# Score and maximum pairs issued in runs of three, with a third score bank taken from the shared PSUM banks

## The reference

```python
# attention: 16 heads of 16, blocks of 128 tokens; a query block sees its own, the previous and the next block
scores = einsum('bhnqd,bhnkd->bhnqk', qb, kwin) * (1 / sqrt(256))
scores = where(|kpos - qpos| <= 128 and 0 <= kpos < 512, scores, -1e30)
out = softmax(scores) @ vwin; out = out @ Wout + bout
x = layernorm(x + out)
# feed-forward with weights rounded to -1, 0, 1
h = relu(x @ Wq1.T + b1)      # 256 -> 1024
x = layernorm(x + h @ Wq2.T + b2)
```

## Time and profile before

| | us |
|---|---|
| median of three runs (1227.03 to 1229.11) | 1227.82 |
| the profiled execution's own time | 1229.44 |
| its span | 1227.7 |
| granted TensorE clock, mean share of full speed | 0.927 |

### The profile page before, as it was taken

The page is one execution under the profiler, slowest core; times in us unless marked ns, Lnnn a source line. Parts: engine busy times, 40 slices in busy tenths (PEclk is TensorE's granted clock), DMA queues, the critical chain, the costliest instruction groups (busy, mean ns, idle before and its releaser), DMA issues.

```text
span 1227.7 us, 28104 instructions
## 1 busy us (share of the span) xinstructions
PE 1074.5 (88%) x8132; PEld 794.1 (65%) x8132; DVE 861.3 (70%) x2934; ACT 611.0 (50%) x1258; POOL 520.0 (42%) x824
## 2 busy tenths in 40 slices
PE   4778998989898899989899998998999899897956
PEld 3445666767666676766667676666767666675746
DVE  2977768777776777777677777768777776777433
ACT  4255545545454554555455454545545454554521
POOL 2233453435445343544534354453435445344430
PEclk8688899998989999898989989899998989899988
DMA  6644424444342444434244443424444342442000
GB/s 173 94 70 71 71 39 86 70 78 64 66 69 40 79 71 78 65 65 69 41 73 76 78 63 66 69 35 81 74 78 62 67 69 35 62 79 37 19 18 18
DMA packets 56924, 80.51 MB, mean 66 GB/s; under 512 B 7729, under 2 KB 27697, under 8 KB 56882
## 3 DMA queue, kind: packets, MB, share of 16 engines
q1 hardware_dynamic: 56882, 80.00, 38.5%
HBM read 20.19 MB, written 8.39 MB: 23 GB/s over the span
## 4 chain that ended last, share of the span: by engine, by line
PE 69%; DVE 10%; issue 7%; ACT 4%; DMA 3%; POOL 3%; SPq 2%; DVEq 1%; POOLq 1%; ACTq 0%
PE shared L517 11%; PE shared L609 11%; PE shared L498 11%; PE st_a L473 11%; PE shared L596 10%; PE st_b L473 4%; PE shared L592 3%; DMA k_stack<-qk_lo 3%; DVE mx L830 3%; PE shared L527 2%; PE shared L578 2%; DVE x L922 2%; PE mx L489 2%; POOL ln_rstd L1036 1%; SPq L388 1%
## 5 line engine op out<-in xcount | busy, mean ns | idle before, releaser
L830 DVE CUSTOM_DVE_ANT_0 mx<-mx,band 128x384 f32<-128x384 f32 (+1 forms) x1024 | 480.8, 512 | 218.7 <-PE mx L489 215.4
L684 ACT ACTIVATE probs<-st_a 128x384 f32<-128x384 f32 (+1 forms) x384 | 202.1, 526 | 357.6 <-PE st_a L473 355.4
L489 PE MATMUL mx<-k_stack,q_stack 48*128 48x384 f32 (+1 forms) x1024 | 280.9, 373 | 14.1 <-DVE rmax L830 11.5
L997 POOL TENSOR_SCALAR_AFFINE_SELECT probs<-probs 128x512 f32<-128x512 f32 (+1 forms) x256 | 129.8, 531 | 333.6 <-ACT probs L684 333.4
L684 ACT ACTIVATE probs<-st_b 128x384 f32<-128x384 f32 (+1 forms) x384 | 201.1, 524 | 0.2 <-PE st_b L473 0.2
L473 PE MATMUL st_a<-q_stack,k_stack 50*128 50x384 f32 (+1 forms) x512 | 185.1, 402 | 4.3 <-ACT probs L684 3.5
L489 PEld LDWEIGHTS mx<-k_stack,q_stack 48*128 48x128 f32 x1024 | 168.9, 199 | 22.7 <-DVE rmax L830 19.7
L517 PE MATMUL shared<-probs,v_aug 128*32 128x384 f32 (+1 forms) x2048 | 154.0, 442 | 0.9 <-issue 0.9
L609 PE MATMUL shared<-w2q,hid_hi 128*128 128x256 f32 x512 | 133.6, 295 | 20.8 <-DVE hid_lo L915 20.8
L596 PE MATMUL shared<-x1T_hi,w1q 128*128 128x256 f32 x512 | 151.2, 310 | 0.0
L596 PE MATMUL shared<-x1T_lo,w1q 128*128 128x256 f32 x512 | 147.8, 306 | 0.0
(11 more groups left out here) (107 smaller groups left out, 1955.7 us busy)
## 6 DMA issues: line engine op xcount, KB each, us to landing
q_stack<-qk_hi SPq DMA_DIRECT2D x128, 128.0 KB, 4.3
k_stack<-qk_hi SPq DMA_DIRECT2D x128, 128.0 KB, 5.3
x_raw<-in_xT SPq DMA_DIRECT2D x16, 512.0 KB, 5.1
q_stack<-qk_lo SPq DMA_DIRECT2D x64, 128.0 KB, 3.9
k_stack<-qk_lo SPq DMA_DIRECT2D x64, 128.0 KB, 5.4
y<-in_x SPq DMA_DIRECT2D x16, 512.0 KB, 5.9
out<-x SPq DMA_DIRECT2D x32, 256.0 KB, 2.1
probs<-in_w2T SPq DMA_DIRECT2D x1, 1024.0 KB, 10.5
```

Of the source, the lines that this page charges most:

```text
L489: mm = pe.matmul(PMX[i % N_MAX][:, col:col + n], SQ[rows, hd, W * m:W * m + W], SK[rows, hd, k0:k0 + n], start=True, stop=True)
L684: act.activation(PR[:, v % 2, g // 2, lo:lo + n], PST[i % 2][:, 0:n], ACT.Exp, scale=SCALE) \
L830: mx = dve.tensor_tensor_reduce(ps, ps, band, 1.0, -3e38, ALU.add, ALU.max, RMAX[:, g, m:m + 1])
L997: pool.affine_select(out=pr_before, in_=pr_before, compare_op=ALU.is_ge, fill=0.0, base=0, pattern=[[0, n], [1, W]], channel_multiplier=-1)
```

## The change

A third score bank is added, the shared banks become two, and the weave puts the units in runs of three. The waits of `scores` on the exponentials follow the number of banks.

```diff
@@ -69,11 +69,12 @@
 N_MAX = 3
-RUN = 2
+N_SCORE = 3
+RUN = 3
 RUNS_AT = (0.5, 0.92)
...
-N_SHARED = 6 - N_MAX
+N_SHARED = 8 - N_MAX - N_SCORE
...
-        PST = [bank("st_a"), bank("st_b")]
+        PST = [bank(f"st{i}") for i in range(N_SCORE)]
...
-                if not (at == 0 and v == 0 and i < 2):
-                    pe.wait_ge(s_exp, 12 * (4 * b + v) + i - 1)
+                if not (at == 0 and v == 0 and i < N_SCORE):
+                    pe.wait_ge(s_exp, 12 * (4 * b + v) + i - N_SCORE + 1)
...
-                    mm = pe.matmul(PST[i % 2][:, col:col + n], SK[rows, hd, W * m:W * m + W],
+                    mm = pe.matmul(PST[i % N_SCORE][:, col:col + n], SK[rows, hd, W * m:W * m + W],
...
-                act.activation(PR[:, v % 2, g // 2, lo:lo + n], PST[i % 2][:, 0:n], ACT.Exp, scale=SCALE) \
+                act.activation(PR[:, v % 2, g // 2, lo:lo + n], PST[i % N_SCORE][:, 0:n], ACT.Exp, scale=SCALE) \
```

## The result

| | before | after |
|---|---|---|
| median of the runs, us | 1228.14 (4 runs) | 1426.67 (1424.38 to 1430.92, 4 runs) |
| ratio of after to before | | 1.162, 95% interval 1.159 to 1.165 |
| span of the profiled execution | 1227.7 | 1424.7 |
| granted TensorE clock, mean | 0.927 | 0.898 |

The kernel is 198.5 us slower. The direction was forecast with 0.94; the size was not: 1356 us with a range of 1290 to 1400. The true time lies 27 us above the range.

What follows compares the result with a forecast made beforehand. TensorE's in-order queue, waiting mostly on shared banks VectorE reads last, sets the time. About 13 us new idle less 2.5 and shortened waits gives 8.3 a period: 116 us over 14 steps plus 12 at the ends, 1356 us; range 1290 to 1400.

Steps and rivals of the forecast that it cites:

- (c): Two shared banks instead of three: each side step waits until the step two before is read out, covered by one step's matmuls.
- The forecast's new waits: TensorE's waits on shared-bank readings and the z sum grow from 6 us a period to 15 or more, some at new places.
- Rival 3: Shared banks are not the bound; the array-change saving and 1.1 us at qk0 remain: 1174 us, chance 5%.
- Step (a): Small-array runs on TensorE: a run of three takes 0.96 us; fewer array changes save 2.5 us a period.
- estimate with no saving: Whole kernel if fewer array changes save nothing because reading PSUM is the bound: 1391 us.
- Step (b): Third score bank: TensorE's waits for a score bank do not appear in the period, so it brings nothing.
- the walk through part 0: First part of a period, steps followed through engine queues: pva at 468.1, ot0 474.8, qk1 477.0, op0 482.5, op1 485.1.
- the term for more low clock: TensorE's clock in the period: the fall taken as before, lasting to about 507, with no further fall added.
- (d): VectorE's and ScalarE's orders: VectorE often has three maxima, 1.76 us, before a reading; negative maxima add 0.66.
- The low-clock stretches stay one a period: Sign expected in the trace after: TensorE's clock falls once a period, as before.
- rival 2: More clock falls, with TensorE also idle before pva in part 0: up to 3.4 us a period, 1404 us, chance 11%.
- the three maxima ahead of a reading: VectorE's queue: three maxima, 1.76 us, stand before its reading of a shared bank, so TensorE's next step waits.

## Why the prediction was right and wrong

**The direction and the mechanism (c) were right.** With two shared banks each step waits for the one two before it. The run with two score and two shared banks and runs of two shows it as cause: 173 us for one bank with everything else kept. The forecast's new waits before pva, ot0, qk1, op0, op1, x1t1, f1(0,0), f1(1,0), f1(1,2) and f2(1) are all in the trace, and the waits grew to 19.5 us a period where 15 or more were named. Rival 3, a gain, is excluded. A wait that the prediction did not name stands before ot1, for v_next (1.1 us).

**Step (a) was nearly right for the run itself:** from 502.09 (the ordinary matmul before the run) to 503.44 three ordinary steps and a run take 1.35 us, so the run 0.99, with 0.96 forecast. The saving in busy time is 26 us, with 35 forecast (14 x 2.5). But runs of three on two shared banks are 25 us slower than runs of two, so it is more than given back as idle. The prediction's estimate with no saving, 1391 us, made by the section "PSUM Bottleneck" of the Trainium skill's "TensorEngine Tiling (Array Packing)" (packing speeds TensorE, not the reading of PSUM), was nearer than the forecast and still 36 us short.

**Step (b) was right only as I used it.** The bank brings nothing to runs of two (1401.8 and 1401.4). For runs of three it does: without it, even with one shared bank more, the time is 1440.5. That TensorE never waited for a score bank before, in runs of two, says nothing of runs of three.

**The step that failed is the walk through part 0, and in the sum the term for more low clock, which was put at nothing.** In the period shown the walk is 4.5 us short by op0.
- The first maximum of a part: VectorE ends the aggregates at 528.1 and starts the maximum at 528.87, idle in between without a releaser other than issue. I had it start at once. But the trace before has the same idle: the aggregates end at 465.51 and the maximum starts at 466.31, though its matmul (465.03, 0.43 us) was done. In both traces it stands in eleven periods, at the start of a step of the loop. 0.8 us; no run takes it away by itself, so its size rests on the trace (the first line is of the kernel before, the second after):

```profile
466.31 0.57 DVE L830 CUSTOM_DVE_ANT_0 mx<-mx,band 128x384 f32<-128x384 f32 x1 [0.79 <-PE mx L489]
...
528.87 0.57 DVE L831 CUSTOM_DVE_ANT_0 mx<-mx,band 128x384 f32<-128x384 f32 x1 [0.79 <-issue]
```

- The copy on GpSimd behind the mask of unit 5. The prediction listed (d) as VectorE's and ScalarE's orders and never walked GpSimd's queue. 17 us in all (8 to 24), shown by undoing it.
- "The low-clock stretches stay one a period". In the thirteen periods there were 15 stretches before and there are 31 after, one to four a period, and 195 us against 96; in the whole execution 288 us against 178. This is rival 2, to which I gave 0.11 and which I priced at up to 3.4 us a period. Its price is not settled: the fillers in the kernel before give 0.2 us for 1 us of low clock, in part 0 after 13.5 us for 69 us, again 0.2 (both with the fillers' own cost in them), and the order with the readings first 0.47 (99 us for 209). For 110 us more of low clock that is 22 to 52 us, 1.7 to 4 a period with 13 periods.

The 70.6 us between 1356 and 1426.7 are thus 17 (shown) and 22 to 52 (from the price of low clock in other kernels), and about 9 for VectorE's late first maximum (0.8 x 11, from the trace). The ranges cover it, but they are not independent, and with the first two taken away as well as I could (1396 us) 40 us remained.

The profile gives a second account, of where the time went and not of what each cause would give back if it were undone. The forecast has TensorE's idle grow by 8.3 + 2.5 = 10.8 us a period, 163 us with the ends, and its busy time fall by 35. Idle grew by 169, so the forecast of the waits was near as a total; busy time grew by 28, and that is 63 of the 69 us by which the profiled execution exceeds the forecast for it. Some 37 of them are work at half rate (by the clock in the trace TensorE is busy at 1.2 GHz for 163 us before and 237 after, and half of the difference is lost), and 9 are saving of (a) that did not come. The last 17 stay open. Busy times rest on the modelled ends of matmuls, so these are estimates.

**A reason that was only half right:** the walk blamed the three maxima ahead of a reading. They are as long as the three exponentials ahead of ScalarE's half (1.76 and 1.36 + 0.64 us). With shorter maxima the reading waits fall from 222 to 176 us, with the reading put first to 153, so for some steps the maxima are the reason. But TensorE's waits for hid_lo before pva (21.8 us in all) and at f2(1) (23.5), and for qk_lo at x1t1 (26.3), are the same to 0.1 us in all three kernels: there ScalarE's queue or the reading itself is late too. That the start times of the walk after part 0 came out right doesn't tell these apart. What is shown is the bank; how the waits divide between the two queues is not.

## What to carry to other kernels

When buffers are dealt out in turn, count how many steps lie between a step and the next user of its buffer, and compare the matmuls in between with the whole reading chain, both engines' queues included: here one buffer less cost 14% of the kernel's time. When a weave moves, walk every in-order queue past the moved instructions, GpSimd's too, even if nothing on it was edited. If a change adds idle to a TensorE-bound kernel, add the clock's fall to the sum and not to the rivals, and try fillers in the longest idle: eleven matmuls a period without a purpose made the kernel before 1.7% faster. When an order changes, look also at what the moved operation now runs beside.

## What the runs showed of the hardware

- A wait of 0.40 us inside a run of small-array matmuls cost 0.75 us in the time to the next step.
- The fall of the clock is not tied to one idle place: with the idle before ot0 and ot1 filled, it came behind the wait before pva instead, 526 to 538 in place of 540 to 548.
- One microsecond at 1.2 GHz cost 0.2 us in two comparisons (both with fillers) and 0.47 in one; none of them changes the clock alone.
- A VectorE operation of 16 columns, mostly 0.18 us in that kernel, took 2.26 us beside a GpSimd addition of 2.35 us.
- At the start of eleven periods VectorE stood idle for 0.79 to 0.84 us between the aggregates and the first maximum, in the kernel before as in the one after; in the periods at both ends it was 0.05 to 0.50 us.
